# First attention of a vision tower: where TensorE multiplies the mixed tokens by the value weights

## The reference

```python
h = _L0_tok_ref(x, L0_tok_w, L0_tok_b, 16)        # patches (196 x 768) @ w.T + b
h = h + _L0_attn_ref(_layernorm(h, axis=-1), L0_attn_Wq, L0_attn_Wk, L0_attn_Wv)
# _L0_attn_ref: tokens quantised to 8 bits by row, weights to -1/0/1
q, k, v = _bitlinear(x, Wq), _bitlinear(x, Wk), _bitlinear(x, Wv)
scores = jnp.einsum('bqd,bkd->bqk', q, k) * B ** (-0.5)      # causal mask, softmax
return jnp.einsum('bqk,bkd->bqd', attn, v)
```

## Time and profile before

| what | value |
|---|---|
| median of 3 runs | 1897.94 us |
| profiled execution, its own time | 1896.8 us |
| its span (first to last instruction) | 1895.0 us |
| mean granted TensorE clock | 0.929 of full |
| busy share: PE, DVE, ACT, POOL | 88%, 62%, 57%, 62% |
| first stage | some 460 us from the start |

### The profile page before, as it was taken

One profiled execution on the slowest core, in us unless ns is written; L12 is line 12 of the kernel. 1 busy time (PEld: TensorE's weight loads), 2 busy tenths in 40 slices (PEclk: granted clock), 3 DMA queues, 4 the chain that ended last, 5 costly groups with the idle time before them and its releaser, 6 DMA issues. The chain is left out here.

```text
span 1895.0 us, 44995 instructions
## 1 busy us (share of the span) xinstructions
PE 1663.5 (88%) x13253; PEld 1212.7 (64%) x13254; DVE 1181.9 (62%) x4868; ACT 1075.5 (57%) x2574; POOL 1168.5 (62%) x1172
## 2 busy tenths in 40 slices
PE   4999999984479873899999999999994999999995
PEld 2666566653456552466666666666662999998985
DVE  2899888883742003588888888888854333444442
ACT  2666666652445432476777777767751555555553
POOL 2455555532068875127767767767666687878876
PEclk8999999995579887699999999999997999999998
DMA  8999999932023334201211111111112454545543
GB/s 199 240 226 231 220 229 228 228 81 61 0 57 68 67 52 95 76 27 47 57 51 53 53 50 53 53 50 52 44 41 66 64 72 66 72 66 69 71 67 38
DMA packets 257798, 172.42 MB, mean 91 GB/s; under 512 B 25598, under 2 KB 250656, under 8 KB 257632
## 3 DMA queue, kind: packets, MB, share of 16 engines
q1 hardware_dynamic: 206432, 134.16, 28.8%
q0 software_dynamic: 50112, 35.64, 13.7%
q10 hardware_dynamic: 1088, 0.53, 0.1%
HBM read 117.64 MB, written 52.40 MB: 90 GB/s over the span
## 5 line engine op out<-in xcount | busy, mean ns | idle before, releaser
L2378 POOL DMA_INDIRECT out_dram<-r_yw,r_idx x212 | 331.0, 1561 | 94.8 <-issue 59.7
L2260 POOL DMA_INDIRECT rows_scratch<-routed_row,slot_u x256 | 252.7, 987 | 169.4 <-DVE slot_u L2199 106.4
L2443 ACT ACTIVATE r_hT<-r_p_up,r_b1T 128x256 f32<-128x256 f32 x424 | 191.4, 473 | 123.8 <-PE r_p_up L2418 120.3
L1925 ACT ACTIVATE a_probsT<-a_p_sc 98x392 f32<-98x392 f32 x384 | 170.4, 500 | 110.8 <-PE a_p_sc L1682 72.3
L2418 PE MATMUL r_p_up<-r_xgT,r_w1e 128*128 128x256 f32 x848 | 222.2, 385 | 9.2 <-DVE r_w1e L2458 8.5
L2406 PEld LDWEIGHTS r_p_y<-w_all,r_hT 128*128 128x128 f32 x1696 | 222.7, 192 | 11.0
L2406 PE MATMUL r_p_y<-w_all,r_hT 128*128 x1696 | 223.4, 275 | 0.0
L449 PE MATMUL p_embed<-pix,w_pix 96*128 96x392 f32 x512 | 207.0, 511 | 3.5 <-ACT pix L570 3.5
L2030 DVE TENSOR_REDUCE a_negmax<-a_p_max 98x2 bf16<-98x392 f32 x256 | 132.3, 558 | 61.6 <-PE a_p_max L1647 61.6
L2418 PEld LDWEIGHTS r_p_up<-r_xgT,r_w1e 128*128 128x128 f32 x848 | 146.2, 192 | 22.7 <-issue 8.3
L723 POOL TENSOR_SCALAR vare<-mv 98x4 f32<-98x4 f32 x64 | 29.9, 468 | 200.6 <-DVE mv L708 174.5
(11 more groups left out here) (378 smaller groups left out, 4091.5 us busy)
## 6 DMA issues: line engine op xcount, KB each, us to landing
img<-in_x_dram SPq DMA_DIRECT2D x192, 196.0 KB, 4.3
img<-in_x_dram SPq DMA_DIRECT2D x192, 189.0 KB, 4.5
r_xg<-rows_scratch SPq DMA_DIRECT2D x106, 130.0 KB
xn_scratch<-xn SPq DMA_DIRECT2D x32, 196.0 KB
h_scratch<-h SPq DMA_DIRECT2D x32, 196.0 KB
h<-h_scratch SPq DMA_DIRECT2D x32, 196.0 KB
h3b<-h_scratch SPq DMA_DIRECT2D x32, 196.0 KB
out_dram<-h SPq DMA_DIRECT2D x32, 196.0 KB
```

The lines of the kernel that those rows point to most:

```text
L1925: act.activation(probsT[:, u % 2, i, :], p_sc[i % 2][:, 0:2 * PAIR], ACT.Exp).then_inc(exped, 1)
L2260: pool.indirect_dma_start(rows_dram, bass.IndirectOffsetOnAxis(ap=slot_u[:, u % ROWS, c, t:t + 1], axis=0), row[:, u % ROWS, c, t, :], Non ...
L2378: pool.indirect_dma_start(acc_dram, bass.IndirectOffsetOnAxis(ap=idx[:, (k - 3) % 4, t:t + 1], axis=0), yw[:, (k - 3) % 4, t, :], None, co ...
L2443: act.activation(hT[:, (k - 1) % 2, f, :], p_up[f][:, 0:G], ACT.Silu, bias=b1T[:, bass.ds(e * FC + f, 1)]).then_inc(act_h, 1)
```

## The change

Patch 6 and patch 7 are issued ahead of the product with the value weights, not behind it. Nothing else moves: no instruction is added or taken away, and all waits are the same.

```diff
                     last.then_inc(mixed, 1)
                 patch(n, k, [5])
+                patch(n, k, [6])
+                patch(n, k, [7])
                 if live(n, 3, UNITS):
                     u = n - 3
                     wait(pe, mixT_ready, u + 1)
...
                                          mixT[:, (k - 3) % 2, t * TILE:(t + 1) * TILE], wv_t[:],
                                          start=True, stop=True)
                     last.then_inc(projected, 1)
-                patch(n, k, [6])
-                patch(n, k, [7])
                 if live(n, 4, UNITS):
```

## The result

The changed kernel takes 1913.86 us (median of 4 runs, 1912.05 to 1916.56), the kernel before 1897.39 in the same comparison: ratio 1.008, 95% interval 1.0063 to 1.0098. The profiled execution took 1913.64 us with a span of 1911.9, against 1896.8 and 1895.0. The forecast was 1912 for the median and for the profiled execution. The change costs 16 us, 0.8%.

A forecast was written before the change was run, and what follows sets the result against it. A closed loop via `hT` (12.20 us a step) was taken as the bound; the loop through DVE would become longer, 12.77. 27 x 0.57 = 15.4, less 0.2, on 1896.8 gave 1912 us; range 1905 to 1919.

The forecast's parts named there:

- Loop A: First stage, from `xn` to `xn` by way of `hT`: sets the pace at 12.20 us before, shrinks to 11.54.
- The value product starts 1.24 us later: PE in each step: its first pass starts at 216.53, not at 215.29, behind patch 6 and 7.
- `hT` and its transposes come earlier, for nothing: ACT and PE: `hT` starts 1.0 us earlier, its transposes 0.66 earlier, held by PE's own queue.
- Loop B: First stage, from `xn` to `xn` through value product and DVE: 11.53 us before, 12.77 after, +0.57 a step.
- DVE sits 1.45 us for the value product: DVE after the maxima, ahead of `rinv`: a wait of 1.45 us a step, where before it was 0.2 to 0.4.
- 27 steps: Steps 3 to 31 less two lengthened by POOL's constants, where the delay costs nothing: 27 x 0.57 = 15.4 us.
- rival 3: First stage: PE's gap of about 1.8 us a step lowers the clock; some 18 us more, 1930 us; chance 3%.
- a clock below 1.00 in the stage: One of the listed signs, in the first stage, that would show the forecast wrong.
- The tail and the later stages: Behind the steady steps: delay passed on whole; later stages, whose clock is not constant, may add or take some 3 us.
- Rival 1: First stage: PE paces, only the way by `hT` matters; a step takes 11.54, -17.8 us, 1879 us; chance 5%.
- Rival 2: First stage: no difference, 1897 us, since DMA engines pace it or DVE's path is some tenths shorter; chance 8%.

The follow-up runs named there:

- e3: The kernel before, with PE's transposes of `xn` moved behind the scores and nothing else: 1884.0 us, ratio 0.993.
- e5b: The kernel before, with one spare DVE addition (98x512) a step, behind the statistics of the residual sum: 1903.2 us, ratio 1.0022.
- e1: Half of the change against the kernel before: patch 6 ahead of the value product, patch 7 behind it: 1895.9 us, ratio 0.9991.
- e6: The changed kernel, with POOL's making of the selection masks moved from its step 16 to its step 34: 1909.2 us.
- e5: The changed kernel, with one spare DVE addition (98x512) at the end of DVE's step, behind the statistics of the residual sum: 1948.6 us.
- e4: The changed kernel, with one spare DVE addition (98x512) a step, between `xd` and the row maxima of the scores: 1916.2 us.
- e8: e7 with ACT making `hT` ahead of the exponentials of the first image: 1872.6 us, ratio 0.9855 to the kernel before.
- e2: The changed kernel, with PE's transposes of `xn` moved behind the scores: 1885.1 us, ratio 0.9933 to the kernel before.
- e7: e2 with POOL's selection masks made late as in e6: 1881.6 us, ratio 0.9911 to the kernel before.
- e8b: e8 run a second time, nothing changed: 1873.3 us, ratio 0.9875 to the kernel before.

## Why the prediction was right

Step by step, by its own terms:

- *Loop A sets the pace before.* Right, to within 0.1: e3, which takes PE's wait for `xn` out of it, gives 12.00 for the 12.05 expected, and e5b's added work in DVE's path costs the usual step nothing. In e1 and e5b both loops end together, at 12.07 and 12.14, so loop A is at most that long there. In e5b that is 0.06 under 12.20 with PE's order unchanged; that DVE's wait for `hcur` itself has this price is argued from the rows (DVE starts 0.10 us after the end of ACT's copy where it waited, 0.05 in e5b) and not tested.
- *The value product starts 1.24 us later.* Its distance from patch 5 went from 0.74 to 2.00: 1.26.
- *`hT` and its transposes come earlier, for nothing.* Right. The transposes start at 211.35, 1.25 behind the value product's start for the 1.22 forecast, held by PE's own list, and `hcur` is ready 1.2 us before DVE takes it. In 17 of 25 steps `hT` itself still waited for the embedding, 0.23 in the rows shown, where I had it start with the end of the exponentials.
- *Loop B becomes the longer one: 12.77.* Measured 12.72. The term that was mis-sized is the value product up to its release, 1.15 by the earlier trace rows and 1.08 now: behind a dense stream its eight passes end sooner after their start.
- *DVE sits 1.45 us for the value product.* 1.54, and 0.78 in the steps where POOL clears tiles or makes constants.
- *27 steps.* The count was right, but the second long step is where the prediction failed: it said the delay would be absorbed there, and the step grew by 1.97 us. POOL was indeed waited for 0.4 us less (1.25 for 1.67). But PE was idle now for 2.7 us and not for 1.8, and behind the gap the clock was at half for some 3.4 us. This is rival 3, with a chance of 3% and the whole stage in view; it came true in one step, at 2.0 us where the prediction had reckoned with up to 6 for a step, and with it one of the prediction's own signs of being wrong, a clock below 1.00 in the stage. e6 took the gap away and the low clock with it. The Trainium skill says of waits between bursts of matmuls, under "HAM oscillation — how this bites in real kernels" in "TensorE: Matmul & The Clock Gate", that they can throttle the engine each time round; here it was one step of 29, and six in e5.
- *The tail and the later stages.* Not in the sum but within its 3 us: +2.0 and -1.7.

So 15.2 us were forecast for the profiled execution and 16.8 came. Misses of opposite sign cancel in part: -1.1 us in the 27 steps (14.1 for 15.2), +2.0 in the long one, +0.6 ahead of them, +2.0 in the tail and -1.7 behind it. The mechanism is right step by step; that the total came within 2 us is partly luck.

Rival 1, PE's pace alone, is out for this kernel: e4 and e5 put the same instruction on both sides of `rinv` and got 0 and 0.61 us. But its sign is right for e8, where the studied order gains. The rule of the Trainium skill that was quoted for it ("Perfetto Trace Analysis", "Identifying the Most-Contended Engine") picks PE in all of these kernels by busy time (305.9 of 320 us before, 290.2 after, between 60 and 380); in the order of the kernel before it misled, and the move paid only once the other loops had been cut. Rival 2's first half, the DMA as the pace, was out at 12.7 us a step; even at 11.7 (e8) no engine waits for an image, and the waits for stores are not shown to be the DMA's load.

## What to carry to other kernels

When several engines run fixed lists, write down each closed loop with its length and its spare time before moving an instruction: a move takes from one loop and gives to another, and it pays only up to the point where the second becomes the longer, here half of the move. The wait that an edit removes tells what it can gain only if no other loop has less to spare than the edit adds. An edit that loses may be the right one after the loop it lengthened has been cut: the same swap cost 16 us first and brought 11 us in the end.

## What the runs showed of the hardware

- The granted clock fell to its lower level (1.2 GHz) after an idle gap of PE of 2.7 us (after), of 1.82 us in e1 and not of 1.78 at the same place before, after 1.90 us in e2 and not after 1.91 in e7, and in e5 after some of many equal gaps of 1.75 us and not after others. e4 and e5b have one such fall each, behind gaps of 2.90 and 2.10 us, and e8 one behind 1.48. So the length of the gap alone does not say it in these rows. In e1, e5 and the changed kernel the step grew by 1.6 to 2.0 us each time. The usual gaps of the changed kernel, 1.15 us, left the clock at 1.00.
- Eight passes of 128 columns released their reader 1.15 us after the first one's start when they had waited, and 1.08 behind a dense stream.
- DVE's statistics started 0.05 us after the end of ACT's copy `hcur` where DVE was still at work when it ended (e5b), and 0.10 after it where DVE had been waiting.
- A store of `h` (98x512 elements) took 5.1 us from issue to landing with the DMA share at 0.93 to 0.96 (before) and 5.0 with 0.95 to 1.02 (e8b), on the median.
